# The second edge loop gathers 127 of a tile's 128 rows with GpSimd and fetches the last one with SyncE

## The reference

```python
feat0, feat1 = (features of each node, 32 scalars and 32 vectors of 3, after a small matrix)
e0 = feat0[edge_src]; e1 = feat1[edge_src]        # one row of 128 numbers for each edge
h  = gelu(gelu(edge_scalar_attr @ W_mlp1) @ W_mlp2)  # 8 numbers of each edge, "radial"
w00, w01, w10, w11 = h @ Wp_00, h @ Wp_01, h @ Wp_10, h @ Wp_11
mid = products of w.., e0, e1 and the four numbers of edge_attr
n   = segment_sum(mid, edge_dst)                  # back to the nodes
y   = cos * self + sin * (n @ W2)
```

## Time and profile before

| | |
|---|---|
| time, median of two runs | 4747.33 us (4743.5 and 4751.16) |
| span of the profiled execution | 4739.3 us |
| second edge loop in it | about 2618 to 4668 us |
| POOL busy | 3526.2 us, 74% |
| DVE busy | 3943.6 us, 83% |
| PE busy | 3573.2 us, 75% |
| ACT busy | 2149.4 us, 45% |
| mean granted clock of PE | 0.963 |

### The profile page before, as it was taken

How to read it: one execution, slowest core, us unless ns; L and a number is a source line. 1 busy time by engine, 2 the same in 40 slices (tenths; PEclk the granted TensorE clock), 3 DMA queues, 4 the chain that set the end, 5 groups by cost and what they waited for, 6 DMA issues and landing times. The chain is left out here.

```text
span 4739.3 us, 94508 instructions
## 1 busy us (share of the span) xinstructions
PE 3573.2 (75%) x16055; PEld 2271.9 (48%) x16055; DVE 3943.6 (83%) x9690; ACT 2149.4 (45%) x6581; POOL 3526.2 (74%) x3353
## 2 busy tenths in 40 slices
PE   4777777777777777777767777877777777777776
PEld 2333433334344333434345555555555555555555
DVE  5998998998999989999988777777777777777776
ACT  2666666666666666666643222222222222222222
POOL 3777777777777777777756677777777777777774
PEclk7999999999999999999989899999999999999999
DMA  6444444444444444444411222222222222222221
GB/s 191 125 121 125 124 121 125 124 122 125 125 121 124 125 121 125 124 125 122 130 35 38 78 55 55 56 56 56 55 54 55 56 55 56 55 55 55 55 56 50
DMA packets 448082, 430.21 MB, mean 91 GB/s; under 512 B 247916, under 2 KB 339824, under 8 KB 447354
## 3 DMA queue, kind: packets, MB, share of 16 engines
q1 hardware_dynamic: 344698, 216.78, 17.5%
q0 software_dynamic: 103168, 211.49, 17.1%
HBM read 411.13 MB, written 16.78 MB: 90 GB/s over the span
## 5 line engine op out<-in xcount | busy, mean ns | idle before, releaser
L423 POOL DMA_INDIRECT attn_xl_rows<-xl,attn_idx x1612 | 1813.6, 1125 | 521.7 <-issue 491.1
L959 POOL DMA_INDIRECT conv_rows<-feat,conv_idx x1612 | 1558.4, 967 | 511.8 <-issue 488.5
L975 PE MATMUL conv_sums_ps<-conv_vals,conv_onehot 128*128 128x256 f32 x3224 | 836.0, 404 | 430.7 <-DVE conv_vals L1068 425.1
L1006 ACT ACTIVATE conv_scaled<-conv_w_ps,conv_edge 128x64 f32<-128x64 f32 x1612 | 374.8, 315 | 1446.9 <-PE conv_w_ps L982 1446.9
L975 PEld LDWEIGHTS conv_sums_ps<-conv_vals,conv_onehot 128*128 128x128 f32 x3224 | 598.4, 195 | 658.8 <-issue 576.7
L1057 DVE TENSOR_TENSOR conv_dots<-conv_rows,conv_edge 128x384 f32<-128x384 f32 x403 | 224.9, 558 | 480.1 <-DMA conv_rows<-feat,conv_idx 479.9
L492 ACT ACTIVATE attn_far<-c_iota,c_minus_pos 128x128 f32<-128x128 f32 x1612 | 515.1, 390 | 10.2
L444 PE MATMUL attn_pre_ps<-attn_attrT,c_W_e 128*128 128x512 f32 x806 | 475.6, 673 | 48.3 <-DMA attn_xr_win<-xr_parts 48.3
L551 DVE TENSOR_TENSOR_SCAN attn_prefix<-attn_limit,attn_prefix,attn_logit_ps 8x512 f32<-8x512 f32 x403 | 508.3, 1261 | 0.0
L474 PE MATMUL attn_stackT_ps<-c_ident,attn_stack 72*128 72x72 f32 x1612 | 191.9, 243 | 417.0 <-DVE attn_stack L578 416.6
L562 DVE TENSOR_TENSOR_SCAN attn_stack<-attn_limit,attn_prefix 8x512 f32<-8x512 f32 x403 | 486.2, 1207 | 0.1
(11 more groups left out here) (137 smaller groups left out, 5972.1 us busy)
## 6 DMA issues: line engine op xcount, KB each, us to landing
attn_attrT<-in_attrT SPq DMA_DIRECT2D x403, 256.0 KB
attn_rel<-rel_group SPq DMA_DIRECT2D x403, 126.0 KB
attn_xl_rows<-xl,attn_idx POOLq DMA_INDIRECT x1612
conv_rows<-feat,conv_idx POOLq DMA_INDIRECT x1612
conv_radial<-in_radialT SPq DMA_DIRECT2D x806, 8.0 KB
attn_xr_win<-xr_parts SPq DMA_DIRECT2D x403, 31.5 KB
attn_limit<-limit SPq DMA_DIRECT2D x403, 16.0 KB
attn_idx<-in_src_tiles SPq DMA_DIRECT2D x403, 2.0 KB
```

Source lines behind the costliest of these rows:

```text
L423: pool.indirect_dma_start(xl_rows[:, b, t, :], None, q["xl"][:, :], bass.IndirectOffsetOnAxis(ap=idx[i][:, t:t + 1], axis=0)).then_inc(row ...
L959: pool.indirect_dma_start(rows[:, k.slot(NX), t, :], None, q["feat"][:, :], bass.IndirectOffsetOnAxis(ap=idx[b][:, t:t + 1], axis=0)).then ...
L975: last = nc.tensor.matmul(to, onehot[:, g.slot(2), t, :], vals[:, g.slot(2), t, :], start=wins > 1 or t == 0, stop=wins > 1 or t == TG - 1)
L1006: nc.scalar.activation(scaled[:, g.slot(2), t, :], w_ps[:, g.slot(2), t, 0:2 * MUL], ACT.Copy, scale=edge4[:, bass.ds(g.index(TG, t), 1), ...
```

## The change

In the second edge loop each of the four gathers of a group takes the rows of edges 0 to 126 of its tile. The row of edge 127 is fetched by SP: it loads the four node numbers of a group from partition 127 of `idx` into registers, and issues four direct transfers of one row each (512 bytes), two groups behind its loads. These count on a semaphore of their own, `last_gathered`, and DVE waits for it as well before its first product. `idx_loaded` and `radial_loaded` become one semaphore, `inputs_loaded`, which reaches 48 for one use; POOL, PE and SP's new step wait for it. All else is as before, the sizes of the rings too.

```diff
-        idx_loaded = [sem(f"idx_loaded{b}") for b in range(ND)]
-        radial_loaded = [sem(f"radial_loaded{b}") for b in range(ND)]
+        inputs_loaded = [sem(f"inputs_loaded{b}") for b in range(ND)]
         rows_gathered = [sem(f"rows_gathered{b}") for b in range(NX)]
+        last_gathered = [sem(f"last_gathered{b}") for b in range(NX)]
...
         @block.sync
         def _(sp):
...
+            def last_rows(k):
+
+                sp.wait_ge(inputs_loaded[k.slot(ND)], k.uses(ND, 48))
+                sp.sem_inc(pool_turn, 1)
+                if not isinstance(k.i, int) or k.at >= NX:
+                    sp.wait_ge(vals_ready, k.back(NX).uses())
+                    sp.sem_inc(pool_turn, 1)
+                _, nodes = nc.values_load_multi_w_load_instructions(idx[k.slot(ND)][P - 1:P, 0:TG], engines=(mybir.EngineType.SP,), min_val=0, max_val=N - 1,
+                                                                        skip_runtime_bounds_check_because="node numbers are below N, and the DMA checks its own address")
+                for t, node in enumerate(nodes):
+                    sp.dma_start(rows[P - 1:P, k.slot(NX), t, :], q["feat"][bass.ds(node, 1), :]).then_inc(last_gathered[k.slot(NX)], 16)
+
+            def body(k, live):
+                if live(0):
+                    loads(k)
+                if live(2):
+                    last_rows(k.back(2))
+
+            def loads(k):
+                b = k.slot(ND)
+                at_least(sp, rows_gathered[k.back(ND).slot(NX)], k.back(ND).uses(NX, 16 * TG))
+                sp.sem_inc(pool_turn, 1)
+                sp.dma_start(idx[b][:, :], q["src_tiles"][:, bass.ds(k.index(TG), TG)]).then_inc(inputs_loaded[b], 16)
+                at_least(sp, hid1_ready, k.back(ND).uses())
+                for half in range(2):
+                    sp.dma_start(radial[half * RADIAL:(half + 1) * RADIAL, b, :],
+                                 q["radialT"][:, bass.ds(k.index(GE, half * HE), HE)]).then_inc(inputs_loaded[b], 16)
+            steps(sp, G, PEEL, U, 2, body)
...
-                pool.wait_ge(idx_loaded[b], k.uses(ND, 16))
+                pool.wait_ge(inputs_loaded[b], k.uses(ND, 48))
...
-                    pool.indirect_dma_start(rows[:, k.slot(NX), t, :], None, q["feat"][:, :],
-                                            bass.IndirectOffsetOnAxis(ap=idx[b][:, t:t + 1], axis=0)
+                    pool.indirect_dma_start(rows[0:P - 1, k.slot(NX), t, :], None, q["feat"][:, :],
+                                            bass.IndirectOffsetOnAxis(ap=idx[b][0:P - 1, t:t + 1], axis=0)
                                             ).then_inc(rows_gathered[k.slot(NX)], 16)
...
-                        pe.wait_ge(radial_loaded[k.slot(ND)], k.uses(ND, 32))
+                        pe.wait_ge(inputs_loaded[k.slot(ND)], k.uses(ND, 48))
...
                         dve.wait_ge(rows_gathered[g.slot(NX)], g.uses(NX, 16 * TG))
+                        dve.wait_ge(last_gathered[g.slot(NX)], g.uses(NX, 16 * TG))
```

More of the change, by code:

```diff
@@ L933, in _ @@
             sp.dma_start(edge4[:, :, :], q["edge4_tiles"].rearrange("p (t c) -> p t c", c=4)).then_inc(edge4_loaded, 16)
-            def body(k, live):
-                if not live(0):
-                    return
+            def last_rows(k):
[8 more added lines that the diff above has]
+                    sp.dma_start(rows[P - 1:P, k.slot(NX), t, :], q["feat"][bass.ds(node, 1), :]).then_inc(last_gathered[k.slot(NX)], 16)
+            def body(k, live):
+                if live(0):
[3 more added lines that the diff above has]
+            def loads(k):
                 b = k.slot(ND)
                 at_least(sp, rows_gathered[k.back(ND).slot(NX)], k.back(ND).uses(NX, 16 * TG))
-                sp.dma_start(idx[b][:, :], q["src_tiles"][:, bass.ds(k.index(TG), TG)]).then_inc(idx_loaded[b], 16)
+                sp.sem_inc(pool_turn, 1)
+                sp.dma_start(idx[b][:, :], q["src_tiles"][:, bass.ds(k.index(TG), TG)]).then_inc(inputs_loaded[b], 16)
                 at_least(sp, hid1_ready, k.back(ND).uses())
@@ L943, in body @@
                     sp.dma_start(radial[half * RADIAL:(half + 1) * RADIAL, b, :],
-                                 q["radialT"][:, bass.ds(k.index(GE, half * HE), HE)]).then_inc(radial_loaded[b], 16)
-            steps(sp, G, PEEL, U, 0, body)
+                                 q["radialT"][:, bass.ds(k.index(GE, half * HE), HE)]).then_inc(inputs_loaded[b], 16)
+            steps(sp, G, PEEL, U, 2, body)
         @block.gpsimd
```

## The result

The changed kernel takes 7326.28 us (7325.47 to 7327.1), the kernel before 4747.33 us: a ratio of 1.544, 95% interval 1.539 to 1.548. The forecast was 4745 us with a range from 4560 to 5150 us. It is wrong, and by far: the time rose by 2579 us where no change was expected.

A forecast was written before the change was run, and what follows sets the result against it. POOL's gathers in the second edge loop were taken to bound the kernel. POOL 0 to -12 us, start +1, end 0 to +4 and SyncE 0 gave -2 us: forecast 4745 us, range 4560 to 5150 us.

The forecast's parts named there:

- The pace: Second edge loop: POOL's gathers set the pace, 5.09 us a group, 3.87 us gathering and 1.22 us between gathers.
- The price of a gather of 127 rows: POOL in the second loop: a gather of 127 rows takes 967 ns, with ends from 277 to 1924 ns.
- Where the bytes go: Second loop's gathers: on one engine the rows land 3.8 us later, hidden; 0 to 4 us once at the end.
- Rival 2: POOL's work on a gather grows when not cut into 16 equal parts: 5000 to 6290 us; chance 0.17.
- Rival 3: POOL writes one engine's list instead of sixteen, so SyncE sets the pace: 4350 or 4590 us; chance 0.21.
- Rival 4: All gathers go to one and the same engine, 16.1 us a group: +4430 us, 9180 us; chance 0.05.
- SyncE: SyncE's queue in the second loop: 5.02 us of work a group, ends 4.11 and 6.02, hidden beside POOL's 5.09.
- The waits: Second loop: waiting for all three inputs costs POOL about 1 us at the start; DVE's extra wait, 0.09 us, is hidden.
- Range and chances: Whole kernel: 8 in 10 from 4560 to 5150 us; faster 0.21, same 0.42, slower 0.37.
- The sign that the prediction named for rival 2: POOL's gather in the second loop: a median over 1050 ns would show that POOL's work on a gather grows.

The follow-up runs named there:

- the run with SyncE's part alone: The changed kernel, but POOL gathers all 128 rows and SyncE's fetched rows land in an unread tile: 4755.47 us, ratio 1.0014 to the kernel before.

## Why the prediction was wrong

**The pace.** Right, and it is why the loss came through undiminished: POOL's gathers end to end set the second loop. Each nanosecond on a gather is 1.6 us of time, and +1598 ns gave +2578 us.

**The price of a gather of 127 rows. This step failed.** The prediction said "127 has no divisor: the work may be cut up differently", kept ends of 277 and 1924 ns, and took 967 ns, "the value nearest to hand". It is 2565 ns in the mean, 1598 ns more, which no term of the sum holds. The upper end was the first loop's slowest gather, a row that knows nothing of the cut: no row bounded this from above. The row taken as a guide, SyncE's issues of 126 and 128 partitions, was of another kind of queue, and 126 is not 127: by the counts that ran, POOL too takes 126 rows almost for the price of 128.

**Where the bytes go.** Right as an alternative, and priced for the wrong resource. The rows of the whole gather do go to one engine, as the Trainium skill has it for 127 partitions in "DMA: Bandwidth & Descriptors", section "Why a DMA increments its semaphore by 16 and not by 1". The trace agrees, with 16 packets of rows a gather, of which one is under way for 69% of the loop's time, and 272 packets in all. It lands 7.9 us after its issue, 5.4 us after POOL's end of 2542 ns; the prediction's "3.8 us later", on 1.7 us, makes 5.5. That this is hidden held too. But the prediction carried the consequence only to the transfer. The lists for the other 15 engines grow to the same length, 127 entries instead of 8, and POOL's time on the gather grows with them, by 13.4 ns for each entry of one list.

**Rival 2, POOL's work grows,** is what happened, with a chance of 0.17 and prices up to 6290 us. "Nothing in the profile speaks for or against" was nearly true: the earlier trace rows and 1612 gathers give 32 packets each, two for each engine, so the lists could have been seen to be per engine, but not that they stay equal in length where the rows don't divide.

**Rival 3, a lighter POOL** with "one engine's list to write instead of sixteen", had the sign wrong: there are always sixteen. **Rival 4, one and the same engine,** is out. In the changed kernel the packets with rows take 3.72 us of engine time a gather, 14.9 us a group, more than the 11.5 us that a group lasts, so one engine can't have carried them all. The trace doesn't name a packet's engine, so that the engines are taken in turn is not shown.

**SyncE.** 5.02 us a group was forecast, 4.08 measured with POOL undisturbed, just under the low end of 4.11. The register load of four numbers took 472 ns, not 1.34 us with its steps: the four address steps were counted twice, once there and once in the 0.46 us of a fetch, and further numbers cost 13 ns each, not 100. A fetch took 1.63 / 4 = 0.41 us. The load after its address, alone:

```profile
L942 SPq TENSOR_LOAD <-conv_idx x403: 468/472/544, 2616.5 to 4674.9; - x135
```

In the changed kernel SyncE does take (4628 - 2614.6) / 403 = 5.00 us. That this is near the forecast's 5.02 is luck: by the sums of their durations against the run with SyncE's part alone, the register load takes 0.29 us a group more, the issues of the four fetches 0.33 and those of the two radial transfers 0.23, as told at the end.

**The waits.** Right: the merged semaphore and DVE's second wait cost 7 us together with SyncE's work. **Range and chances:** slower had 0.37, and slower through POOL 0.17. The range ended at 5150 us, since it took in the lower part of that case only, and even the case's highest price, 6290 us, was 1036 us short. The sign that the prediction named for rival 2, a median over 1050 ns, is there with 2542.

## What to carry to other kernels

Keep the row count of an indirect gather at a multiple of 16 (64 and 128 ran here). By the eight counts that ran, POOL's price is about 0.87 us plus 13 ns for each entry of the longest list, and that list has rows / k entries, with k the largest divisor up to 16: 128 rows make 8, 127 make 127, 126 make 9. Dropping rows from a gather saves next to nothing (64 rows 907 ns, 128 rows 944 ns), so rows handed to another engine buy next to nothing on POOL even where the count stays a multiple of 16. When a transfer is cut up anew, price not only where the bytes go but also who writes the lists.

## What the runs showed of the hardware

POOL's time on a gather:

| rows | engines with rows (k) | entries of the longest list | median, ns |
|---|---|---|---|
| 64 | 16 | 4 | 907 |
| 128 | 16 | 8 | 944 |
| 120 | 15 | 8 | 982 |
| 126 | 14 | 9 | 987 |
| 61 | 1 | 61 | 1661 |
| 122 | 2 | 61 | 1661 |
| 113 | 1 | 113 | 2356 |
| 127 | 1 | 127 | 2542 |

Beside the long lists, register loads of other engines take longer. DVE's load of one number took 307 ns and takes 514 ns in the median with 127 rows and nothing new on SyncE; SyncE's load of four numbers took 472 ns alone and takes 783 ns in the changed kernel. The changed kernel, then the run with 127 rows alone:

```profile
L941 SPq TENSOR_LOAD <-conv_idx x403: 471/783/1338, 2621.2 to 7216.2; - x135
```

```profile
L1039 DVEq TENSOR_LOAD <-c_tile_block x403: 303/514/1054, 2647.2 to 7254.3; - x135
```

With 61 entries DVE's median is 308 ns again, its longest 693; with one long gather in four it is 724. SyncE's issues grow too: a fetch's median from 228 ns alone to 262 in the changed kernel, its longest from 274 to 894. What the loads and issues share with the lists was not tested.

PE's mean granted clock fell from 0.97 to 0.69 in the second loop, PE waiting 2150.8 us there for DVE instead of 422.0, and its sums went from 404 to 647 ns a matmul. No loss of time is seen from it: POOL waited only 4.0 us in all for DVE's values in that loop.
